# Rotary partners fetched by transfers between partitions, with four smaller moves, in a decoder layer on one core

## Chip, cores and metric

The kernel runs on 1 core of one Trainium2 chip. The metric is device microseconds of one execution, as the median of several.

## What is computed

One decoder layer over 32 sequences of 128 tokens and width 128, with a context of 77 rows for each sequence.

```python
x = x + attn(layernorm(x), rotary on q and k, 16 heads of 8, softmax) @ Wp + bp
x = x + cross_attn(layernorm(x), ctx)              # 16 heads of 8, 77 keys
x = x + ffn(layernorm(x))
# rotary: q*cos + rot(q)*sin, rot swaps the two features of each pair and negates one
# ffn: top 2 of 8 experts (128 -> 512 -> 128, gelu), weighted by a softmax of the two
#      logits, then layernorm(input + sum) * gamma + beta
```

## The kernel before

Features lie on partitions for the projections, tokens on partitions for everything between. Sequences are taken in 8 groups of 4, so that a projection is one product over 512 columns.

**The 64 steps.** One loop over STEPS does attention. A step is one sequence of self-attention or one of cross-attention; from step 13 to step 50 the two kinds alternate, then only cross-attention is left. Each engine has its own program of the same steps, and `plan()` (L97) is the table that says in which step a group's other work falls: `put` places a product with its evictions in a step and a turn (ITEMS), `job` a piece of work of SP, ACT, DVE or POOL (JOBS). All engines work in order. They meet at semaphores alone.

In a step n, TensorE (PE) does, in order: `shifted(st, 0)`, which writes the shifted scores of two of four row tiles and beside them the raw scores of step n+2; `rows_turned` of step n-2 (L891); filler products where the step has no projection (`dense`, L978, 3 or 6 of them); the turned maxima of step n+1 (L879); the second half of the values of step n-1 (L873); the items of turn 1 (projections, L921 among them); `projected` of step n-2 (L898, L899); `shifted(st, 1)`; `sums_turned` of step n-1 (L886); filler; the first half of the values of step n. `sums_turned` waits for ACT's copy of the sums and, because it writes where the projection was, for DVE's residual of step n-2 (L1346).

In a step DVE does: two maxima of step n+2 (L1319), its part of the items of turn 1, the residual of step n-2, two more maxima, `norm_rows` of step n-1 (L1328, L1330), which waits for `sums_turned` and is what `rows_turned` of the next step waits for, and then the statistics of step n-2. ACT does two exponentials (L1140), some copies, its part of the items, and two more exponentials.

**Rotary.** For each group g and for q and k there are two products over 512 columns: one with the weights, one with the weights' columns swapped in pairs (`rq`, `rk`). DVE adds the bias to each and multiplies with the cosine or the sine (L1368), out of PSUM into `ra` and `rb`. POOL adds the two (`turned`, L1775), ACT makes the high half in f16 (`high_part`), POOL the low half (`low_part`, L1780), and SP parks both in DRAM and spreads them over the rows that the scores need (`park_q`, `spread_q`, L627 and L637). For groups 4 to 7 the q product is in step 11, 18, 26 and 34 and the k product in the step behind it; the sum is in the same step, high, low and park one and two steps later, the spread three steps later.

**Hand-over.** In the last steps the first 40 tiles of the experts are laid out: the routed rows of group 5 are scattered to DRAM by POOL (L1860), two in each of the steps 60 to 63 (place 0 and 1 in `scatters`), and DVE builds the table `tab` in four pieces, the last one (`first_entries`, L1507 to L1479) at the start of step 63. SP loads a tile of 128 routed rows (L721) only when all scatters of groups 4 and 5 have landed and `tab` is there. PE turns a loaded tile (L1080), DVE copies it, and the expert's products follow (L1069, L1095), three tiles deep; `expert_turns` drives all engines, `between(i)` puts the rest of the attention between the turns.

**Last stage.** Eight chunks of four sequences: PE sums the two expert outputs of each token into one of eight PSUM banks (L1121), DVE takes statistics (L1688, L1691) and the negated mean (L1693), POOL makes the inverse deviation and the product (`inverse_deviations`, L1956 to L1960), ACT normalizes (L1289), DVE, and POOL in chunks 1 and 3, multiplies with gamma (L528), and DVE adds the rest (L1711).

Of the kernel before, what the change touches and what calls it, by code (L numbers as in the profile page):

```python
# [30 lines left out]
GS = 4  # L31
# [39 lines left out]
BETA = 3  # L71
NA = ((EARLY + 1) * TOK * TOPK - E * (P - 1)) // P // ROUND * ROUND
# [28 lines left out]
def plan():  # L101
# [14 lines left out]
    for g in range(NG):  # L116
        own = SELF_STEP[g * GS + GS - 1]
        if g >= 2:
# [17 lines left out]
            job(made + 2 if g == 3 else made + 3, "spread", g)  # L136
# [27 lines left out]
        if chosen < NS:  # L164
# [5 lines left out]
            for i in range(GS):  # L170
                for k in range(TOPK):
                    job(chosen + 1 + i, ("scatter", k), (g, i, k))
# [33 lines left out]
def decoder_layer(nc, x, ctx_t, w_self, b_self, bp, w_cross, b_cross, bo, wg, bg, w1, b1, w2, b2,  # L206
# [3 lines left out]
    with stack:  # L210
# [230 lines left out]
        s_rhi = sem("s_rhi")  # L441
        s_route = sem("s_route")
# [80 lines left out]
        LAST = CHUNKS - 1  # L523

# [72 lines left out]
        def _(sp):  # L597
# [88 lines left out]
            for n in range(NS):  # L686
# [18 lines left out]
                for g in jobs_at(n, "load_x"):  # L705
                    load_x(g)
                if n == 20:
# [64 lines left out]
        def _(pe):  # L772
# [211 lines left out]
            def step(st):  # L984
# [114 lines left out]
            def between(i):  # L1099
                if i == -3:  # L1100
# [17 lines left out]
            for n in range(CHUNKS):  # L1118
# [6 lines left out]
        def _(act):  # L1125
# [41 lines left out]
            def work(name, g):  # L1167
                bank, c = item(name, g)
                w = BANKS[bank]
                if name in ("q", "rq", "k", "rk", "log", "pos", "cnt"):  # L1170
                    return
                act.wait_ge(s_w[bank], c)
                if name == "xnt":
# [111 lines left out]
            for i in range(SEQS):  # L1285
                if i % FC == 0:
                    act.wait_ge(s_rsfm, i // FC + 1)
                r = SUM[i // FC][:, (i % FC) * D:(i % FC + 1) * D]
                act.activation(xn3all[:, i * D:(i + 1) * D], r, ACT.Identity,  # L1289
# [3 lines left out]
        def _(dve):  # L1293
# [63 lines left out]
            def work(name, g):  # L1357
# [4 lines left out]

# [185 lines left out]
            def step(st):  # L1548
# [33 lines left out]
                if st.at == COUNTED + 2:  # L1582
                    first_sums()
# [101 lines left out]
            def chunk_statistics(n):  # L1685
                dve.wait_ge(s_add, n + 1)
                for i in range(FC):
                    V.bn_stats(stf[:, n * FC + i, :], SUM[n][:, i * D:(i + 1) * D]).then_inc(s_rawf, 1)  # L1688
# [3 lines left out]
                dve.wait_ge(s_stf, (n + 1) * FC)  # L1692
                V.tensor_scalar(nmf[:, n * FC:(n + 1) * FC], mvf[:, n * FC:(n + 1) * FC, 0], -1.0, None, ALU.mult).then_inc(s_nmean, 1)  # L1693
# [33 lines left out]
        def _(pool):  # L1727
# [42 lines left out]
            def turned(g, k):  # L1770

                for name in (("q", "rq"), ("k", "rk"))[k]:
# [270 lines left out]
```

## Time and profile before

| | |
|---|---|
| median of 3 runs | 603.55 us (601.19 to 603.73) |
| the profiled execution | 598.75 us |
| its span, first to last instruction | 596.9 us |
| busy, share of the span: PE, PE's weight load, DVE, POOL, ACT | 87%, 65%, 65%, 58%, 54% |
| start of step 0, of step 63, of the first expert product, of the last stage's first sum | 28.6, 376.2, 389.7, 565.4 us |

The span is that of the profiled execution. Microseconds in the text count from its start. An engine's idle time has a cost only where PE or another engine of the chain waits for what comes late.

### The profile page before, as it was taken

Reading aid. Unit: us, or ns where it says so; the run is one execution under the profiler, and the core shown is the slowest. Engines: PE = TensorE matmul, PEld = TensorE weight load, DVE = VectorE, ACT = ScalarE, POOL = GpSimd, SP = SyncE. Lnnn points to the kernel's source line nnn. Section 1 sums busy time; section 2 is a strip of 40 time slices with the busy share of each in tenths; the row PEclk is TensorE's granted clock in tenths of the full one; section 3 lists DMA queues with packets and bytes.
Section 4 is the critical chain, followed back from the end, with each engine's and each line's share of the span. In section 5 each row is a group of like instructions: output and inputs, shape, how many; then the busy total and the mean of one; then the engine's idle time right before and its main releaser. Section 6 shows DMA issues by size and latency. Waiting matters only on the chain.

```text
span 596.9 us, 21959 instructions
## 1 busy us (share of the span) xinstructions
PE 519.3 (87%) x7657; PEld 389.0 (65%) x7658; DVE 385.3 (65%) x1275; ACT 324.3 (54%) x870; POOL 347.1 (58%) x475
## 2 busy tenths in 40 slices
PE   6889998989998998888979998789888899999980
PEld 4456565656655655665657676588877799999530
DVE  5778887777886786685855766544644444445096
ACT  2447565766766666665656465445434455555143
POOL 5748597636438748638573467546554554444374
PEclk8999999999999999999999999889999999999995
DMA  5232340431762403403112210022222222222393
GB/s 155 84 115 71 104 152 28 151 91 52 226 230 87 137 20 87 137 25 102 34 40 74 80 47 25 28 55 60 64 68 80 74 69 57 57 57 59 98 252 88
DMA packets 68785, 52.57 MB, mean 88 GB/s; under 512 B 8752, under 2 KB 65077, under 8 KB 68690
## 3 DMA queue, kind: packets, MB, share of 16 engines
q1 hardware_dynamic: 62994, 41.92, 25.1%
q0 software_dynamic: 4352, 8.53, 4.4%
q8 instruction: 59, 0.97, 0.7%
q10 hardware_dynamic: 1344, 0.85, 0.5%
q14 instruction: 36, 0.29, 0.2%
HBM read 33.10 MB, written 18.64 MB: 87 GB/s over the span
## 4 chain that ended last, share of the span: by engine, by line
PE 57%; issue 11%; DVE 9%; DMA 7%; ACT 6%; SPq 5%; POOL 4%; DVEq 0%; ACTq 0%; POOLq 0%
PE S L1069 8%; PE AV L873 7%; PE AV L1095 4%; PE SM L1095 4%; PE ST L841 4%; PE W L921 4%; PE ST L847 4%; PE SM L886 3%; ACT prob L1140 3%; PE AV L978 3%; PE SM L898 2%; DVE nmp L1319 2%; SPq L637 2%; PE W L934 2%; PE SM L891 2%
## 5 line engine op out<-in xcount | busy, mean ns | idle before, releaser
L1140 ACT ACTIVATE prob<-ST 128x512 f32<-128x512 f32 (+1 forms) x256 | 138.4, 592 | 117.3 <-PE ST L847 111.1
L1319 DVE TENSOR_REDUCE nmp<-S 128x4 bf16<-128x308 f32 (+1 forms) x251 | 134.6, 576 | 15.8 <-PE S L797 10.0
L1269 ACT ACTIVATE va<-S,b1s 128x128 f32<-128x128 f32 x284 | 81.1, 369 | 81.0 <-PE S L1069 66.8
L1931 POOL DMA_INDIRECT expert_out<-va,ks x71 | 70.0, 985 | 73.4 <-DVE va L1644 44.7
L1860 POOL DMA_INDIRECT routed<-pay,dest x64 | 65.9, 1029 | 33.3 <-PE ST L847 20.2
L873 PE MATMUL AV<-prob,va 77*32 77x128 f32 (+1 forms) x2048 | 84.4, 280 | 0.6 <-issue 0.5
L1069 PE MATMUL S<-va 128*128 128x128 f32 x568 | 77.7, 280 | 7.6 <-issue 5.5
L841 PE MATMUL ST<-nmt,onesr 32*77 32x128 bf16 (+1 forms) x1024 | 73.7, 219 | 8.9 <-ACT prob L1140 3.3
L1069 PEld LDWEIGHTS S<-va 128*128 128x128 f32 x568 | 70.3, 195 | 10.1 <-issue 8.8
L841 PEld LDWEIGHTS ST<-nmt,onesr 32*77 32x77 bf16 (+1 forms) x1024 | 52.4, 102 | 33.5 <-issue 31.8
L873 PEld LDWEIGHTS AV<-prob,va 77*32 77x32 f32 (+1 forms) x2048 | 49.0, 109 | 24.4 <-issue 20.8
L1828 POOL TENSOR_SCALAR ve<-mv 128x1 f32<-128x1 f32 x64 | 15.7, 245 | 62.2 <-DVE mv L1355 61.7
L886 PE MATMUL SM<-idf,ots 128*128 128x128 f32 x128 | 27.2, 294 | 16.5 <-DVE x L1346 11.3
L1095 PE MATMUL AV<-w2s,va 128*128 x288 | 40.6, 284 | 0.0
L1830 POOL TENSOR_TENSOR rs<-ve,half 128x1 f32<-128x1 f32 x64 | 36.7, 574 | 5.3
L1095 PE MATMUL SM<-w2s,va 128*128 x280 | 39.4, 284 | 0.0
L1644 DVE SCALAR_TENSOR_TENSOR va<-AV,ks 128x128 f32<-128x128 f32 x36 | 12.6, 351 | 40.3 <-remote 15.0
L978 PE MATMUL AV<-onesr,idb 128*128 128x256 bf16 x255 | 38.0, 273 | 0.3 <-ACT x2all L1134 0.3
L847 PE MATMUL ST<-q2s,k2s 32*77 32x128 f16 x512 | 35.8, 214 | 0.0
L1095 PEld LDWEIGHTS AV<-w2s,va 128*128 128x128 f32 x288 | 35.0, 192 | 0.8
L1631 DVE COPY va<-w1s 128x512 f32 x71 | 30.5, 430 | 6.9 <-PE S L1069 5.3
L1095 PEld LDWEIGHTS SM<-w2s,va 128*128 128x128 f32 x280 | 34.0, 192 | 0.7
(278 smaller groups left out, 1133.2 us busy)
## 6 DMA issues: line engine op xcount, KB each, us to landing
ks<-routed SPq DMA_DIRECT2D x72, 65.0 KB
q2s<-q_parts SPq DMA_DIRECT2D x32, 128.0 KB
qs<-q_parts SPq DMA_DIRECT2D x20, 128.0 KB
ks<-k_parts SPq DMA_DIRECT2D x20, 128.0 KB, 2.7
k2s<-k_parts SPq DMA_DIRECT2D x32, 77.0 KB
xin<-x SPq DMA_DIRECT2D x8, 256.0 KB, 3.4
q_parts<-q2part SPq DMA_DIRECT2D x8, 256.0 KB
w1s<-w SPq DMA_DIRECT2D x8, 256.0 KB, 4.4
```

Source lines behind the costliest of these rows:

```text
L841: mm(o, onesr[rows, b, 0:st.keys], nmt[rows, st.at % 2, :], start=True, stop=False)
L847: ins = mm(o, k, q, start=False, stop=True)
L873: last = mm(AV[32 * c:32 * c + 32, m * L:(m + 1) * L], v[0:st.keys, st.group % 2, at:at + VW], prob[0:st.keys, j, b * L:(b + 1) * L], star ...
L886: last = tr(TURNED[:, m * L:(m + 1) * L], ots[:, m * L:(m + 1) * L], idf[:, :])
L978: mm(bank, idb[:, :], some[:, 0:bank.shape[1]], start=True, stop=True)
L1069: last = mm(S[k][:, q * P:(q + 1) * P], w1c[:, k, q * P:(q + 1) * P], xt[:, (c + 1) % 4, :], start=True, stop=True)
L1095: last = mm(o, ht[:, (c - 1) % 4, q, :], w2s[:, bass.ds(e * (HID // D) + q * D, D)], start=False, stop=(q == HC - 1))
L1140: act.activation(prob[0:st.keys, j, :], ST[j % 2][0:st.keys, :], ACT.Exp, scale=SCALE).then_inc(s_exp, 1)
L1269: last = act.activation(ht[:, (c + 1) % 4, q, :], S[k][:, q * P:(q + 1) * P], ACT.Gelu, bias=b1s[:, bass.ds(b + q, 1)])
L1319: V.tensor_reduce(nmp[:, st.at % 2, row_tile(p), 0:NB], bank[:, 0:NB * st.keys].rearrange("p (b k) -> p b k", b=NB), AX.X, ALU.max, negate ...
L1860: pool.indirect_dma_start(out=routed, out_offset=bass.IndirectOffsetOnAxis(ap=dest[:, g % 2, i, k:k + 1].bitcast(U32), axis=0), in_=pay[:, ...
L1931: pool.indirect_dma_start(out=expert_out, out_offset=bass.IndirectOffsetOnAxis(ap=xr[:, at % ROUND, D + 1:D + 2].bitcast(U32), axis=0), in ...
```

## The change

It has five parts.

1. For groups 4 to 7 (SWAP = 4) the products `rq` and `rk` go. ACT moves the q or k product with its bias out of PSUM into `rb`. SP copies it to `ra` with each pair of partitions exchanged, in two transfers of 64 partitions. One step later DVE multiplies `ra` with the sine and `rb` with the cosine (`rotate`, at the end of its step). POOL's sum, the high and low halves, park and spread all come one step later than before.
2. PE's `sums_turned` comes behind filler and values of the step, no longer ahead of them.
3. The scatters of group 5 go three, three and two into the steps 60, 61 and 62; the pieces of `tab` come earlier, the last at the start of step 62.
4. In the first three turns of the experts PE gets two filler products of 512 columns each.
5. In the last stage chunk 0 is summed in two halves, in two banks; the negated mean is made by POOL, no longer by DVE.

```diff
@@ plan()
-                put(at, turn, names[1], g)
+                if g < SWAP:
+                    put(at, turn, names[1], g)
+                else:
+                    job(at, "swap", (g, k))
+                    at += 1
+                    job(at, "rotate", (g, k))
                 job(at, "sum", (g, k))
                 job(at + 1, "high", (g, k))
                 job(at + 2, "low", (g, k))
                 job(at + 2, ("park_q", "park_k")[k], g)
-            job(made + 2 if g == 3 else made + 3, "spread", g)
+            job(made + 2 if g == 3 else made + 3 if g < SWAP else made + 4, "spread", g)
...
+                    n = TOPK * i + k
+                    if g == EARLY:
+                        job(chosen + 1 + n // 3, ("scatter", n % 3), (g, i, k))
+                    else:
+                        job(chosen + 1 + i, ("scatter", k), (g, i, k))
@@ sync
+            def swap(g, k):
+                bank, c = item(("q", "k")[k], g)
+                sp.wait_ge(s_wf[bank], c)
+                sp.wait_ge(s_parts, 2 * (g - 1) + k + 1)
+                sp.dma_start(ra[0::2, k, :], rb[1::2, k, :]).then_inc(s_swap[k], 16)
+                sp.dma_start(ra[1::2, k, :], rb[0::2, k, :]).then_inc(s_swap[k], 16)
@@ tensor, step()
                 shifted(st, 1, after)
+                background(st, 2)
+                values(st, 0)
                 if before:
                     sums_turned(before)
-                background(st, 2)
-                values(st, 0)
@@ tensor, between()
+                if i < 0:
+                    dense(2, ST[1][:, :])
@@ tensor, last stage
-            for n in range(CHUNKS):
+            for m in range(2):
+                at = slice(m * FC // 2 * D, (m + 1) * FC // 2 * D)
+                for k in range(TOPK):
+                    pe.wait_ge(s_y2[k][0], 16)
+                    last = mm((SUM[0], SUM[LAST])[m][:, at], idf[:, :], y2[0][:, k, at], start=(k == 0), stop=(k == TOPK - 1))
+                last.then_inc(s_add, 1)
+            for n in range(1, CHUNKS):
+                if n == LAST:
+                    pe.wait_ge(s_norm, FC)
@@ scalar, work()
+                if name in ("q", "k"):
+                    k = ("q", "k").index(name)
+                    act.wait_ge(s_sum, 2 * (g - 1) + k + 1)
+                    act.activation(rb[:, k, :], w[:, :], ACT.Identity, bias=bqk[:, 2 * k:2 * k + 1]).then_inc(s_wf[bank], 1)
@@ vector
                 if name in ("q", "rq", "k", "rk"):
+                    if g >= SWAP:
+                        return
...
+            def rotate(g, k):
+                dve.wait_ge(s_swap[k], 32 * (g - SWAP + 1))
+                for part, table in ((ra, sinb), (rb, cosb)):
+                    p3 = part[:, k, :].rearrange("p (i l) -> p i l", i=GS)
+                    V.tensor_tensor(p3, p3, table[:, :].unsqueeze(1).to_broadcast([P, GS, L]), ALU.mult).then_inc(s_rot, 1)
@@ vector, step()
                 if st.at == COUNTED + 2:
-                    first_owners()
-                if st.at == COUNTED + 3:
+                    first_sums()
                     first_entries()
...
+                for g, k in jobs_at(st.at, "rotate"):
+                    rotate(g, k)
                 background(st, 2)
                 background(st, 3)
...
                 if st.at == COUNTED + 1:
                     take_tiles()
-                if st.at == COUNTED + 2:
-                    first_sums()
+                    first_owners()
@@ vector, chunk_statistics(): the negated mean goes; gpsimd, inverse_deviations():
-                pool.wait_ge(s_nmean, n + 1)
+                pool.wait_ge(s_stf, (n + 1) * FC)
                 G.tensor_scalar(rsf[:, 1, at], mvf[:, at, 1], 4 * EPS, None, ALU.add).then_inc(s_rsf, 1)
+                G.tensor_scalar(nmf[:, at], mvf[:, at, 0], -1.0, None, ALU.mult).then_inc(s_nmean, 1)
```

On PE, in step 35, where group 7's k is made, before (`xnt,wqk` is the product with the q or k weights, `wcross,onormt` the projection of step 33):

```order
L891 MATMUL SM<-idf,onorm 128x128
L879 MATMUL AV<-idb,nmp 128x128
L873 MATMUL AV<-prob,va 32x128 x8
L921 MATMUL W<-xnt,wqk 128x512 x2
L898 MATMUL SM<-wcross,onormt 128x128
L899 MATMUL SM<-c,three_ones 128x128
```

and now:

```order
L920 MATMUL SM<-idf,onorm 128x128
L908 MATMUL AV<-idb,nmp 128x128
L902 MATMUL AV<-prob,va 32x128 x8
L950 MATMUL W<-xnt,wqk 128x512
L927 MATMUL SM<-wcross,onormt 128x128
L928 MATMUL SM<-c,three_ones 128x128
```

One of the two products of 512 columns ahead of the projection is gone. At the end of the same step, before:

```order
L841 MATMUL ST<-nmt,onesr 77x128 x2
L797 MATMUL S<-k2s,q2s 128x77 x2
L847 MATMUL ST<-q2s,k2s 77x128 x2
L886 MATMUL SM<-idf,ots 128x128 x2
L873 MATMUL AV<-prob,va 32x128 x8
L841 MATMUL ST<-nmt,onesr 128x128 x2
```

and now:

```order
L870 MATMUL ST<-nmt,onesr 77x128 x2
L826 MATMUL S<-k2s,q2s 128x77 x2
L876 MATMUL ST<-q2s,k2s 77x128 x2
L902 MATMUL AV<-prob,va 32x128 x8
L915 MATMUL SM<-idf,ots 128x128 x2
L870 MATMUL ST<-nmt,onesr 128x128 x2
```

The sums' transposition (`idf,ots`) has gone behind the values (`prob,va`), next to the shifted scores of step 36.

On POOL, steps 61 to 63 (`routed` is a scatter; `ve`, `rs`, `pay` are one norm; `gsum` is the first row of the count of group 6, in step 63), before:

```order
L1860 DMA routed<-pay,dest 33920x130 x2
L1828 TENSOR_SCALAR ve<-mv 128x1
L1830 TENSOR_TENSOR rs<-ve,half 128x1
L1841 TENSOR_SCALAR pay<-x2all,mv,rs 128x128
L1860 DMA routed<-pay,dest 33920x130 x2
L1828 TENSOR_SCALAR ve<-mv 128x1
L1830 TENSOR_TENSOR rs<-ve,half 128x1
L1841 TENSOR_SCALAR pay<-x2all,mv,rs 128x128
L1860 DMA routed<-pay,dest 33920x130 x2
L1848 TENSOR_TENSOR gsum<-hotb 128x16
```

and now:

```order
L1893 TENSOR_SCALAR pay<-x2all,mv,rs 128x128
L1912 DMA routed<-pay,dest 33920x130 x3
L1880 TENSOR_SCALAR ve<-mv 128x1
L1882 TENSOR_TENSOR rs<-ve,half 128x1
L1893 TENSOR_SCALAR pay<-x2all,mv,rs 128x128
L1912 DMA routed<-pay,dest 33920x130 x3
L1880 TENSOR_SCALAR ve<-mv 128x1
L1882 TENSOR_TENSOR rs<-ve,half 128x1
L1893 TENSOR_SCALAR pay<-x2all,mv,rs 128x128
L1900 TENSOR_TENSOR gsum<-hotb 128x16
```

The last two scatters of group 5 stood in step 63, directly ahead of the count; now the last two stand ahead of the norm of step 62.

## Rows read from the trace of the kernel before

**Rows 1.** Page, busy time, share of the span, instructions; then granted clock by slices.
```profile
PE 519.3 (87%) x7657; PEld 389.0 (65%) x7658; DVE 385.3 (65%) x1275; ACT 324.3 (54%) x870; POOL 347.1 (58%) x475
...
PEclk8999999999999999999999999889999999999995
```

**Rows 2.** Groups: form, count | busy us, mean ns | idle before, releaser.
```profile
L921 PE MATMUL W<-xnt,wqk 128*128 128x512 f32 x48 | 24.0, 620 | 1.5 <-ACT xnt L1134 1.5
...
L1368 DVE SCALAR_TENSOR_TENSOR rb<-W,bqk,sinb 128x512 f32<-128x512 f32 x14 | 10.5, 748 | 1.4 <-PE W L921 0.5
...
L1192 ACT ACTIVATE q2part<-W,bqk 128x512 f16<-128x512 f32 x8 | 5.5, 687 | 4.9 <-PE W L943 4.9
```

**Rows 3.** Timeline, step 34: start us, us, engine line [idle before].
```profile
217.09 2.06 PE L921 MATMUL W<-xnt,wqk 128*128 128x512 f32 x4
...
218.98 0.38 PE L898 MATMUL SM<-wself,onormt 128*128 128x128 f32 x2
...
219.26 0.74 DVE L1368 SCALAR_TENSOR_TENSOR rb<-W,bqk,sinb 128x512 f32<-128x512 f32 x1
...
220.35 0.41 PE L886 MATMUL SM<-idf,ots 128*128 128x128 f32 x2 [0.37 <-DVE x L1346]
...
221.59 0.29 DVE L1330 TENSOR_TENSOR onorm<-SM,rden 128x128 f32<-128x128 f32 x1
...
221.94 0.33 PE L891 MATMUL SM<-idf,onorm 128*128 128x128 f32 x1
```

**Rows 4.** Waits of PE over the 64 steps: us, times, longest.
```profile
PE SM L886 <- DVE x L1346: 11.3, 19, 1.0
...
PE SM L898 <- ACT onormt L1134: 5.1, 10, 0.9
...
PE SM L886 <- DVE x2all L1346: 3.4, 8, 1.0
```

**Rows 5.** Timeline, step 25, which has filler products and no wait.
```profile
169.34 0.44 PE L886 MATMUL SM<-idf,ots 128*128 128x128 f32 x2
...
169.61 0.49 PE L978 MATMUL AV<-onesr,idb 128*128 128x256 bf16 x3
...
170.25 0.29 DVE L1330 TENSOR_TENSOR onorm<-SM,rden 128x128 f32<-128x128 f32 x1
...
171.17 0.33 PE L891 MATMUL SM<-idf,onorm 128*128 128x128 f32 x1
```

**Rows 6.** Timeline, DVE after steps 19 and 27.
```profile
142.97 0.29 DVE L1346 TENSOR_TENSOR x<-SM,xin 128x128 f32<-128x128 f32 x1 [0.71 <-PE SM L899]
...
183.10 1.29 DVE L1319 TENSOR_REDUCE nmp<-S 128x4 bf16<-128x512 f32 x2 [0.37 <-PE S L797]
```

**Rows 7.** DMA issues: KB, median us to landing.
```profile
ks<-k_parts SPq DMA_DIRECT2D x20, 128.0 KB, 2.7
...
w1s<-w SPq DMA_DIRECT2D x8, 256.0 KB, 4.4
```

**Rows 8.** Timeline, the hand-over to the experts.
```profile
368.92 0.98 POOL L1860 DMA_INDIRECT routed<-pay,dest  x1 [1.14 <-PE ST L847]
...
380.20 0.23 DVE L1479 CAST tab<-x2t 1x160 int32<-1x160 f32 x1
...
380.77 0.41 PE L886 MATMUL SM<-idf,ots 128*128 128x128 f32 x2 [1.45 <-DVE x2all L1346]
...
387.10 0.45 PE L1080 MATMUL W<-idf,ks 128*128 128x128 f32 x1 [2.16 <-DMA ks<-routed]
...
389.65 0.77 PE L1069 MATMUL S<-va 128*128 128x128 f32 x2 [0.98 <-DVE va L1631]
```

**Rows 9.** Chain that ended last, 376 to 396: start us, us, what.
```profile
380.16 3.88 DMA routed<-pay,dest
...
384.19 0.49 SPq L720
```

**Rows 10.** Windows: PE, PEld, DVE, ACT, POOL busy, then granted clock.
```profile
388.00:392.00 4.00, 2.83 (x12) 2.56 (x13) 1.56 (x6) 0.00 (x0) 2.05 (x2) 0.50 0.37 89
```

**Rows 11.** Timeline, the last stage.
```profile
570.46 0.17 DVE L1693 TENSOR_SCALAR xnt<-xnt 128x4 f32<-128x4 f32 x1
...
574.81 1.27 POOL L528 TENSOR_TENSOR xn3all<-xn3all,gammar 128x512 f32<-128x512 f32 x1
...
574.93 1.17 DVE L1693 TENSOR_SCALAR xnt<-xnt 128x4 f32<-128x4 f32 x1
...
576.19 0.70 POOL L1956 TENSOR_SCALAR xnt<-xnt 128x4 f32<-128x4 f32 x1
...
586.93 0.59 POOL L1956 TENSOR_SCALAR xnt<-xnt 128x4 f32<-128x4 f32 x1 [0.33 <-DVE xnt L1693]
```

**Rows 12.** One line, all its instructions: ns min/median/max.
```profile
L1711 DVE TENSOR_TENSOR x2all<-xn3all,x2all x9: 424/691/693, 573.0 to 591.8; 128x512 f32<-128x512 f32 x7, 128x256 f32<-128x256 f32 x2
```

More of the change, by code:

```diff
@@ L71 @@
 BETA = 3
+SWAP = 4
 NA = ((EARLY + 1) * TOK * TOPK - E * (P - 1)) // P // ROUND * ROUND
@@ L441, in decoder_layer @@
         s_rhi = sem("s_rhi")
+        s_swap = [sem(f"s_swap{k}") for k in range(2)]
+        s_rot = sem("s_rot")
         s_route = sem("s_route")
@@ L523, in decoder_layer, with summed @@
         LAST = CHUNKS - 1
+        def summed(i):
+            bank = SUM[LAST] if FC // 2 <= i < FC else SUM[i // FC]
+            return bank[:, (i % FC) * D:(i % FC + 1) * D]
         def times_gamma(eng, first, seqs, s):
@@ L706, in _ @@
                     load_x(g)
+                for g, k in jobs_at(n, "swap"):
+                    swap(g, k)
                 if n == 20:
@@ L1169, in work @@
                 w = BANKS[bank]
-                if name in ("q", "rq", "k", "rk", "log", "pos", "cnt"):
+                if name in ("rq", "rk", "log", "pos", "cnt") or name in ("q", "k") and g < SWAP:
                     return
                 act.wait_ge(s_w[bank], c)
-                if name == "xnt":
+                if name in ("q", "k"):
+                    k = ("q", "k").index(name)
+                    act.wait_ge(s_sum, 2 * (g - 1) + k + 1)
+                    act.activation(rb[:, k, :], w[:, :], ACT.Identity, bias=bqk[:, 2 * k:2 * k + 1]).then_inc(s_wf[bank], 1)
+                elif name == "xnt":
                     move(turned_of(g)[:, :], w[:, :], s_wf[bank])
@@ L1287, in _ @@
                     act.wait_ge(s_rsfm, i // FC + 1)
-                r = SUM[i // FC][:, (i % FC) * D:(i % FC + 1) * D]
-                act.activation(xn3all[:, i * D:(i + 1) * D], r, ACT.Identity,
+                act.activation(xn3all[:, i * D:(i + 1) * D], summed(i), ACT.Identity,
                                bias=rsf[:, 1, i:i + 1], scale=rsf[:, 0, i:i + 1]).then_inc(s_norm, 1)
@@ L1685, in chunk_statistics @@
             def chunk_statistics(n):
-                dve.wait_ge(s_add, n + 1)
-                for i in range(FC):
-                    V.bn_stats(stf[:, n * FC + i, :], SUM[n][:, i * D:(i + 1) * D]).then_inc(s_rawf, 1)
+                for i in range(n * FC, (n + 1) * FC):
+                    dve.wait_ge(s_add, n + 2 if n or i >= FC // 2 else 1)
+                    V.bn_stats(stf[:, i, :], summed(i)).then_inc(s_rawf, 1)
                 dve.wait_ge(s_rawf, (n + 1) * FC)
@@ L1770, in turned @@
             def turned(g, k):
-                for name in (("q", "rq"), ("k", "rk"))[k]:
-                    bank, c = item(name, g)
-                    pool.wait_ge(s_wf[bank], c)
+                if g >= SWAP:
+                    pool.wait_ge(s_rot, 2 * (2 * (g - SWAP) + k + 1))
+                else:
+                    for name in (("q", "rq"), ("k", "rk"))[k]:
+                        bank, c = item(name, g)
+                        pool.wait_ge(s_wf[bank], c)
                 G.tensor_tensor(ra[:, k, :], ra[:, k, :], rb[:, k, :], ALU.add).then_inc(s_sum, 1)
@@ L1865, in scatters @@
                 for g, i, k in jobs_at(n, ("scatter", place)):
-                    pool.wait_ge(s_st[1], NJ // 2 * n + place + 1)
+                    pool.wait_ge(s_st[1], NJ // 2 * n + min(place, 1) + 1)
                     scatter(g, i, k)
@@ L1902, in step @@
                     norm_instance(near(st, -2))
+                scatters(n, 2)
             set_up()
```

4 lines of the change are left out of this document (1 added, 3 removed).

## The prediction

> **What bounds the kernel now.** The page comes first: TensorE (PE) is busy 519.3 us, 87% of the span, and its granted clock is at or near the upper level almost everywhere [rows 1]. So work taken off PE counts in full where PE waits for nothing, and each stretch where it waits has to be read by itself.
>
> For the groups of columns I go to the grouped lines [rows 2]. For the cost of a product I go to the timeline of a step with a rotary product [rows 3]. There both products together (four matmuls) begin at 217.09, and the projection L898 begins at 218.98: PE advances 1.89 us for two, 0.95 us each by the starts and 1.03 by the row's own 2.06; I take 0.97. Behind them the same rows show the second limit. DVE does the second bias and sine out of PSUM, 0.74 us, then the residual, and `sums_turned` (L886) waits 0.37 us for it. The waits over the 64 steps [rows 4] say how often that is: 11.3 us at 19 self steps, 3.4 us at 8 cross steps, and 5.1 us at 10 steps for ACT's `onormt`. In a step with filler and no items [rows 5] PE waits for neither; DVE's norm (L1330) ends at 170.54 and `rows_turned` (L891) starts at 171.17.
>
> Last come the seams: the hand-over to the experts, where PE waits 1.45 us behind DVE's table pieces and 2.16 us for the first routed tile [rows 8], where the chain of waits goes over the last scatter [rows 9] and the clock is 0.50 [rows 10]; and the last stage, where PE is done early and POOL and DVE alternate [rows 11, 12].
>
> **Part 1, eight products less.** 8 x 0.97 = **-7.7 us** [rows 3]. DVE has cover for what comes in their place, with two exceptions:
> - ACT's move with bias: the nearest row is a bias eviction of the same size, 0.69 us [rows 2]. It starts when the product ends, and PE has about 1 us of projection and shifted scores before it needs the bank's or ACT's next result. Nothing.
> - The swap on SP: an issue took 0.49 us [rows 9], so 1.0 us for two. A spread of 128 KB landed in 2.7 us, a load of 256 KB in 4.4 us [rows 7]. From the product's end to `rotate` I count 0.7 + 1.0 + 2.7 to 4.4, that is 4.4 to 6.1 us. DVE comes to `rotate` at the end of the next step: that step begins near 221.94 [rows 3] and takes 5.5 us (64 steps in 353) or a little more, so about 228, 9 us behind the product's end at 219.15. Hidden. POOL's sum, the halves, park and spread come one step later, but group 4's spread then stands in step 15, and its scores are first wanted in step 18, where the later groups have more. Nothing.
> - The two multiplies on DVE. What they replace, two passes of 748 ns [rows 2], lay in front of the residual; they lie at the end of the step, in front of the next maxima. I have no row of a multiply of 128x512 that reads SBUF alone but L1711 of the last stage, an addition: 691 ns [rows 12]. So 1.4 us at each of eight places. Behind steps 19 and 27 DVE has 0.71 and 0.37 us of idle time [rows 6], elsewhere more. The rest is late for the maxima, the residual and so the sums: 1.3 us for group 4, 0.9 for group 5, 0.4 for each of the last two. **+3.0 us.** Bounds: 0 (all in idle time) and 8 x 1.4 = +11.
>
> A rule speaks against the form of the swap. By the Trainium skill ("DMA: Bandwidth & Descriptors", "Rules for kernel authors") two transfers to disjoint halves of the partitions serialize, and one of 128 partitions should be used. No row of this trace has such a pair; by the rule the second lands 2.7 us behind the first, and the sum above does not change, since 7 to 9 us would still be just inside the step.
>
> **Part 2, sums behind filler and values.** In the 8 cross steps of rows 4 the residual is awaited while values could run: -3.4 us. At the 19 self steps nothing is gained. There DVE's chain (residual, maxima, norm, L1328 to L1330) is itself what `rows_turned` waits for: in rows 3 the norm ends at 221.88 and L891 starts at 221.94. In the 28 steps with filler the sums go up to 1.0 us later, and their end plus DVE's 0.76 us for reciprocal and norm then exceeds the old start of L891 by 0.27 us: in rows 5, 171.17 against sums ending near 170.6 plus 0.8 and the hand-overs. 28 x 0.27 = 7.6 us; at the 10 places where PE waits 5.1 us for `onormt` behind ACT's exponentials [rows 4] it is absorbed, about 3. So +4.5 - 3.4 = **+1 us**, with -3 (none of the 7.6) to +6 (a little more than all of it, less the gain).
>
> **Part 3, scatters and table.** The last scatter of group 5 is issued at 380.16 and lands 3.88 us later; then SP issues the tile's load [rows 9], PE waits 2.16 us for it, and PE has waited 1.45 us for the residual, which stands behind the last table cast at 380.20 [rows 8]. With the last scatters one step (5.5 us) earlier they are issued by 374.7 and land at 378.6; the table comes before 375. Both waits are then gone, -3.6. A third scatter at the end of steps 60 and 61 is 1.1 us more on POOL, which idles 1.14 us ahead of the second scatter there [rows 8]. The table pieces stand in front of a residual one step earlier: some of the 1.45 stays. With the four filler products and the clock, which is 0.50 from 384 to 392 [rows 10] behind those waits, I come to **-3.8 us**. Bounds: -2 (only the tile's wait) and -5.6 (clock back early as well).
>
> **Part 4, filler in three turns.** PE waits for a tile or for DVE's copy there (0.98 us before 389.65 [rows 8]), so it lies in idle time; 0, at most 3 x 0.3 = +1. It is in the bounds of part 3.
>
> **Part 5, last stage.** From 572 on, POOL's inverse deviations set the pace: 0.23 to 0.70 us for a small operation [rows 11]. The negation is one more such, 0.2 us or so, in each of six chunks, less the 0.33 us that POOL still waits for DVE at 586.93. But 0.17 us (and 1.17 us, in chunks beside POOL's gamma) go from DVE. Chunk 0 in halves starts the stage sooner by half of its sums, in a stretch where POOL has nothing: taken back later by POOL. **+0.8 us**, bounds -1 and +2.
>
> **The sum.** -7.7 + 3.0 + 1 - 3.8 + 0.8 = -6.7. Against the profiled execution of 598.75 us, whose span is 596.9 us, that is 592.0 us. The execution is 4.8 us below the median of the runs, 603.55 us; taken off the median it is **596.9 us**.
>
> **The rivals.**
> - **A: DVE waits for the swap (slower).** `rotate` stands in DVE's queue, so whatever follows (maxima, residual, norm) waits with it, then PE. It decides if the two transfers land later than about 9 us behind the product. For: the exchange goes by single partitions, and no row shows one. Against: 4.4 us for the largest load in rows 7. Late by 1.5 us at 8 places is +12 on 596.9: 608.9 us.
> - **B: the multiplies stall against POOL.** L1693, 0.17 us as a rule, takes 1.17 us at 574.93 beside POOL's gamma from 574.81 [rows 11]: a small DVE operation that reads and writes SBUF took 1.0 us longer. The multiplies of `rotate` stand where POOL norms a sequence or adds a pair. At three places +3, 600 us; at all eight 604.9.
> - **C: the sums behind the values cost their full 7.6 us**, gains of waits only on paper: 602.4 us, no change.
> - **D: the hand-over gives nothing**, since the next thing there (the residual behind the logits, or the load of the tile) is as late: 600.6 us.
> - **E: everything that hangs on DVE in part 1 is hidden** and the clock comes back early: -12, 591.5 us.
>
> Rival B has a rule beside it. The Trainium skill ("SBUF — State Buffer", "Who interferes with whom") says that DVE and GpSimd share a port pair as an exclusive lock, and that a DVE operation with two inputs from SBUF holds it. By that rule each `rotate` that meets a POOL operation waits for its end, and the reverse; the trace agrees in kind with its 1.17 beside 0.17 us.
>
> **How the numbers follow.** A measurement of this kernel can tell about 0.5%, 3 us, from no change: faster is below 600.5. The forecast has .68, A .05, B .08, C .08, D .05, E .06. Faster is the forecast's, E and the milder half of B and D: 0.77. Same holds C and the rest of B and D: 0.15. Slower is A and the worst of B and C together: 0.08. The bounds of parts 1 to 5 added as independent give about -5 and +6 around 596.9; the range of 8 in 10 is 590.5 to 603.5.
>
> **What would show it.** Right: L921's successor has 32 matmuls in place of 48; PE's time from 28.6 to the first expert product falls by about 8 us; the wait of L886's successor for the residual in cross steps is gone, while `rows_turned` now waits for `onorm` in filler steps; the multiplies take near 0.7 us with no wait for the swap in front; PE's wait for the first routed tile is gone, and the last chunk's times stay. Wrong: idle time of DVE in front of `rotate` (A); multiplies of over 1 us beside POOL (B); waits of `rows_turned` of 0.3 us and more in most steps (C); a wait before the first tile that is still 2 us (D).

## The result and the profile after

| | before | changed |
|---|---|---|
| median of 4 runs | 603.64 us (601.19 to 604.17) | 628.55 us (617.53 to 633.68) |
| profiled execution, its span | 598.75, 596.9 us | 626.57, 624.7 us |
| mean granted clock of the profiled execution | 0.978 | 0.914 |

The changed kernel is slower: ratio 1.031, 95% interval 1.018 to 1.045. Ratios, here and below, are of the fast runs, those within 1.5% of the fastest of their kernel (here two of the four); by the medians it is 1.041. 596.9 us was forecast, with 590.5 to 603.5 as the range. Its runs are 16 us apart and sorted by clock: 617.53 us at 0.939, 626.57 at 0.914, 630.53 at 0.902, 633.68 at 0.899.

The page of the changed kernel, the rows that answer to [rows 1]:

```profile
PE 553.2 (89%) x7651; PEld 409.4 (66%) x7652; DVE 381.5 (61%) x1267; ACT 331.8 (53%) x878; POOL 348.6 (56%) x483
...
PEclk9999899999999998999589755579999899999996
```

PE issues six instructions fewer and is busy 33.9 us longer. The last row gives most of the reason: in slices 20 and 24 to 26 of 40 the granted clock is near 0.5. The windows around the two longest low stretches (columns as in [rows 10]: stretch, length, busy time and count of PE, PEld, DVE, ACT, POOL, then clock, DMA share, GB/s):

```profile
292.00:298.00 6.00, 5.00 (x92) 2.91 (x90) 5.14 (x16) 2.17 (x5) 4.91 (x11) 1.00 0.17 58
298.00:316.00 18.00, 16.70 (x212) 10.67 (x212) 6.90 (x21) 7.96 (x20) 9.64 (x13) 0.53 0.08 24
344.00:350.00 6.00, 4.62 (x96) 3.29 (x93) 2.87 (x10) 2.48 (x7) 4.18 (x7) 1.00 0.65 177
350.00:382.00 32.00, 31.95 (x366) 21.75 (x364) 13.22 (x56) 11.77 (x29) 14.48 (x22) 0.50 0.07 21
382.00:415.00 33.00, 32.33 (x312) 21.83 (x312) 15.13 (x71) 11.80 (x27) 13.53 (x22) 0.50 0.12 33
```

From 350 to 415 us the clock stands at 0.50, the lower of its two levels, 1.2 GHz. PE is then busy all the time (31.95 of 32 us), DVE for 13.22 us of the same 32. A shorter low stretch is at 298 to 316, and windows of 1 us show three more, of 3 to 4 us, at 66, 186 and 237 (a sixth, at 493, lies in the experts' stage). Just ahead of each of the five the timeline of PE has its longest waits:

```profile
66.05 0.23 PE L870 MATMUL ST<-nmt,onesr 32*128 32x128 bf16 x2 [1.77 <-DMA w1s<-k_parts]
...
185.68 0.25 PE L870 MATMUL ST<-nmt,onesr 32*77 32x128 bf16 x2 [1.22 <-ACT prob L1180]
...
236.32 0.23 PE L870 MATMUL ST<-nmt,onesr 32*128 32x128 bf16 x2 [1.40 <-ACT prob L1180]
...
299.30 0.80 PE L927 MATMUL SM<-wcross,onormt 128*128 128x128 f32 x2 [1.49 <-ACT onormt L1174]
...
348.27 0.33 PE L920 MATMUL SM<-idf,onorm 128*128 128x128 f32 x1 [1.38 <-issue]
```

Where the time went, by stretch (a step is counted from one turned maxima, L879 or now L908, to the next; the differences are of the two profiled executions):

| stretch | changed minus before, us |
|---|---|
| ahead of step 0 | -1.1 |
| 16 of the 64 steps, at and behind the low stretches (6, 7, 29, 30, 37 to 39, 50 to 52, 57 to 62) | +29.2 |
| the other steps | -5.6 |
| from there to the first expert product (18.9 us before, 23.1 now) | +4.2 |
| experts to the first sum of the last stage | +1.4 |
| last stage | -0.3 |
| sum | +27.8 |

So the products did go (32 matmuls of L950 in place of 48), and the eight steps that held them are 7.5 us shorter together. The loss lies elsewhere, at and behind the stretches at low clock.

### The profile page after: what moved, and what is told of

Same layout as the page of the kernel before. It is cut to its first block, busy times and chain, and to the rows that moved or that the text cites. A ratio compares the mean times of both kernels' runs of the same rounds, so it can differ in the third digit from the quotient of the medians.

```text
span 624.7 us, 21971 instructions
## 1 busy us (share of the span) xinstructions
PE 553.2 (89%) x7651; PEld 409.4 (66%) x7652; DVE 381.5 (61%) x1267; ACT 331.8 (53%) x878; POOL 348.6 (56%) x483
## 4 chain that ended last, share of the span: by engine, by line
PE 57%; DVE 12%; issue 8%; DMA 7%; POOL 5%; SPq 5%; ACT 4%; DVEq 1%; POOLq 0%; another core or an unknown queue 0%; ACTq 0%
PE AV L902 9%; PE S L1098 7%; PE AV L1007 5%; DVE nmp L1362 4%; PE ST L870 4%; PE SM L1124 3%; PE AV L1124 3%; PE ST L876 3%; ACT prob L1180 3%; PE SM L927 3%; PE W L950 2%; SPq L656 2%; DMA expert_out<-va,ks 2%; PE SM L920 2%; PE SM L915 2%
## 5 line engine op out<-in xcount | busy, mean ns | idle before, releaser
L870 PE MATMUL ST<-nmt,onesr 32*77 32x128 bf16 (+1 forms) x1024 | 83.3, 232 | 14.7 <-ACT prob L1180 9.7
L902 PE MATMUL AV<-prob,va 77*32 77x128 f32 (+1 forms) x2048 | 92.1, 302 | 0.0
L870 PEld LDWEIGHTS ST<-nmt,onesr 32*77 32x77 bf16 (+1 forms) x1024 | 57.2, 111 | 40.4 <-issue 38.7
L902 PEld LDWEIGHTS AV<-prob,va 77*32 77x32 f32 (+1 forms) x2048 | 52.9, 117 | 24.3 <-issue 14.5
L1880 POOL TENSOR_SCALAR ve<-mv 128x1 f32<-128x1 f32 x64 | 15.3, 239 | 71.1 <-DVE mv L1398 69.4
L1007 PE MATMUL AV<-onesr,idb 128*128 128x256 bf16 x255 | 47.4, 321 | 0.7 <-ACT nmt L1174 0.4
L876 PE MATMUL ST<-q2s,k2s 32*77 32x128 f16 x512 | 43.2, 239 | 0.0
L1371 DVE RECIPROCAL rden<-SM 128x16 f32<-128x16 f32 x64 | 16.2, 253 | 40.5 <-PE SM L915 40.5
L1174 ACT ACTIVATE ots<-AV 128x256 f32<-128x256 f32 x64 | 24.9, 390 | 19.9 <-PE AV L902 19.6
L1686 DVE COPY va<-W 128x128 f32<-128x128 f32 x71 | 20.5, 288 | 24.4 <-PE W L1109 20.3
```

What stands on the lines that cost most here:

```text
L870: mm(o, onesr[rows, b, 0:st.keys], nmt[rows, st.at % 2, :], start=True, stop=False)
L876: ins = mm(o, k, q, start=False, stop=True)
L902: last = mm(AV[32 * c:32 * c + 32, m * L:(m + 1) * L], v[0:st.keys, st.group % 2, at:at + VW], prob[0:st.keys, j, b * L:(b + 1) * L], star ...
L1007: mm(bank, idb[:, :], some[:, 0:bank.shape[1]], start=True, stop=True)
```

## The experiments

Theory T, formed on the profile above: `sums_turned` behind the values (part 2) lets PE's small waits run together, and the clock falls behind them. Rival U: eight products less leave PE too little to do, whatever the order. Rival V: the swaps' traffic makes the waits. Later came rival W: the late sums cost the time by themselves and the clock is only a symptom.

### One part undone, one part alone

`e1_sums_ahead` is the change without part 2:

```diff
@@ tensor, step(), of the changed kernel
-                background(st, 2)
-                values(st, 0)
                 if before:
                     sums_turned(before)
+                background(st, 2)
+                values(st, 0)
```

> The changed kernel with its part 2 undone (sums_turned again ahead of filler and values); parts 1, 3, 4, 5 stay. Theory T (the late sums collect PE's small waits into single ones of 1.2 to 1.5 us, behind which the granted clock falls to 0.50 for up to 63 us): the stretches at 0.50 at steps 29, 37, 50 and 57 go, mean clock back to 0.97 or more, time 594 to 600 us. Rival U (eight products less leave PE too little to do, whatever the order): the clock stays at 0.90 to 0.94 and the time above 612. Rival V (the swaps' DMA traffic makes the waits): the same as U.

`e2_no_swap` is the change without part 1:

```diff
-SWAP = 4
+SWAP = 8
```

> The changed kernel with its part 1 undone (SWAP 8: all products for the partners as before); parts 2 to 5 stay. Theory T: the low stretches at steps 50 and 57, far behind the last swap, stay; mean clock 0.90 to 0.95, time 618 to 640 us. Rivals U and V: clock 0.97, time 600 to 608 us.

`e3_sums_late_only` is the kernel before with part 2 alone (the first diff the other way round, on the kernel before).

> The kernel before with part 2 alone. Theory T: slower by 2 to 5%, 615 to 635 us, with stretches at clock 0.50 in the 64 steps. Rivals U and V: 600 to 608 us, the ledger of part 2 alone (+1 us, at most +6), clock 0.97.

Measured on one chip, where the kernel before took 605.63 us: without part 2 596.97 us (593.39 to 599.92), ratio 0.984 (0.976 to 0.992); without part 1 625.05 us, 1.034 (1.025 to 1.042); part 2 alone 619.12 us, 1.014 (1.005 to 1.022). U and V fall with this as the cause of the loss: with the swaps and the eight products less, but the old order, the kernel is faster than before, and with none of them (e2) it is as slow as the change. The loss needs part 2. Alone it costs 1.4% (2.2% by the medians), where T gave 2% to 5% and 615 to 635 us; the rest of e2's 3.4% comes with parts 3 to 5 beside it, and no run says from which of them. The page of `e1_sums_ahead`:

```profile
PEclk9999999899999899999999999999999999999995
```

Its clock is 0.979, but it isn't free of low stretches. Its windows, and the longest wait of PE in the 6 us ahead of the second:

```profile
107.00:110.00 3.00, 3.00 (x24) 2.42 (x15) 2.97 (x12) 1.55 (x6) 2.05 (x4) 0.50 0.34 91
203.00:209.00 6.00, 5.64 (x74) 3.53 (x73) 4.65 (x19) 2.52 (x5) 1.14 (x3) 0.50 0.25 81
```

```profile
199.65 0.23 PE L870 MATMUL ST<-nmt,onesr 32*128 32x128 bf16 x2 [0.38 <-ACT prob L1180]
```

The profile of the kernel before has no low stretch in its 64 steps. So part 1 may have a price in clock of its own; it is small, since the mean clocks of e1's four runs (0.970 to 0.979) are those of the kernel before (0.961 to 0.980). The waits of PE over the 64 steps of `e1_sums_ahead` (us, times, longest):

```profile
PE SM L915 <- DVE x L1389: 11.2, 16, 1.2
PE ST L870 <- ACT prob L1180: 9.0, 20, 1.4
...
PE SM L915 <- DVE x2all L1389: 2.3, 4, 1.0
```

and of the changed kernel:

```profile
PE ST L870 <- ACT prob L1180: 9.7, 22, 1.4
...
PE SM L915 <- DVE x L1389: 2.3, 5, 0.5
```

The waits for the residual have gone from 11.2 + 2.3 to 2.3 us, as the change promises. What the sum of waits doesn't show is what lies behind the sums. At the start of step 57, before:

```profile
339.19 0.44 PE L886 MATMUL SM<-idf,ots 128*128 128x128 f32 x2
...
339.82 0.25 DVE L1328 RECIPROCAL rden<-SM 128x16 f32<-128x16 f32 x1
...
341.49 0.33 PE L891 MATMUL SM<-idf,onorm 128*128 128x128 f32 x1
...
342.91 0.86 DVE L1319 TENSOR_REDUCE nmp<-S 128x4 bf16<-128x308 f32 x2 [2.03 <-remote]
343.07 1.08 ACT L1140 ACTIVATE prob<-ST 77x512 f32<-77x512 f32 x2 [2.69 <-remote]
```

and changed:

```profile
345.88 0.44 PE L915 MATMUL SM<-idf,ots 128*128 128x128 f32 x2
...
347.63 0.26 DVE L1371 RECIPROCAL rden<-SM 128x16 f32<-128x16 f32 x1 [2.47 <-PE SM L915]
...
348.27 0.33 PE L920 MATMUL SM<-idf,onorm 128*128 128x128 f32 x1 [1.38 <-issue]
...
348.60 1.08 ACT L1180 ACTIVATE prob<-ST 77x512 f32<-77x512 f32 x2 [2.87 <-remote]
```

In both kernels DVE and ACT stand idle here for 2.0 to 2.9 us; the trace puts three of the four idle times down to "remote" and names no queue or engine. Of the fourth (2.47 us, changed) DVE spends the last 1.3 us with its input ready: the sums end at 346.32. Before, the norm was over by then (it followed the sums of 339.19), so that PE ran `rows_turned` (341.49) and the rest through the pause. With the sums behind the values the norm comes 1.3 us behind them, and `rows_turned` waits 1.38 us. That is the wait ahead of the 65 us at clock 0.50.

A wait of this length isn't enough by itself, nor is it needed: in e1 the clock fell behind 0.38 us. The kernel before has a wait of 1.43 us at step 11, and its clock stays at 1.00:

```profile
92.00 0.23 PE L841 MATMUL ST<-nmt,onesr 32*128 32x128 bf16 x2 [1.43 <-DMA q2s<-q_parts]
```

What tells these cases apart isn't settled by any run.

### Filler in the waits

If the clock were all, filler products in the five waits would bring the time back while every other engine is as late as before. `f1_fill_five`:

```diff
@@ tensor, step(), of the changed kernel
                 shifted(st, 0, after)
+                if st.at == 57:
+                    dense(8, AV[:, 2 * L:4 * L])
                 if last:
                     rows_turned(last)
...
-                    dense(idle_at(st, 1), AV[:, 2 * L:4 * L])
+                    dense(idle_at(st, 1) + (6 if st.at == 49 else 0), AV[:, 2 * L:4 * L])
...
                 if before:
                     sums_turned(before)
                 background(st, 3)
+                if st.at in (5, 28, 36):
+                    dense(7, AV[:, 2 * L:4 * L])
```

> The changed kernel, late sums and all, with about 1 us of filler products more for PE at the five places where its profile shows a wait of 1.2 us or more just ahead of a stretch at clock 0.50: 7 filler products at the end of steps 5, 28 and 36, 6 ahead of step 49's turned maxima, 8 ahead of step 57's rows_turned. Theory T (the single long wait brings the clock down, the low clock costs the time): the stretches at 0.50 there are gone or short, mean clock 0.96 or more, 596 to 605 us, though no wait of another engine has been shortened. Rival W (the late sums cost the time by themselves, the clock is a symptom): 615 us or more.

`f2_fill_one` has the first of these edits alone.

> The changed kernel with filler at the last of the five places alone (8 products ahead of step 57's rows_turned), where its profile shows the longest low stretch, 350 to 415 us. Theory T: that stretch goes, the other four stay: 605 to 616 us. Rival W: 622 us or more.

They came to a chip on which the kernel before took 581.83 us, 4% less. There f1 took 586.97 us, 1.008 (1.001 to 1.014), and f2 582.37 us, 1.001 (0.996 to 1.007): no answer, since the change itself wasn't run beside them. What differs is in the traces: on this chip no wait of ACT or DVE is put down to "remote" (in the kernel before, on the other chip, 9.0 us of ACT's and 19.9 of DVE's are). I call these chips with and without pauses. So the change went beside its variants twice more.

On a chip without pauses (the kernel before: 579.53 us):

> The changed kernel, unedited, beside its variants on one chip. The last four runs were on a chip whose traces show none of the pauses put down to 'remote' and where the kernel before takes 582 us. Theory T (late sums turn pauses of the other engines into waits of PE, and these bring the clock down): on a chip with pauses 617 to 635 us and clock 0.90 to 0.95; on one without, 578 to 590 us, within 1.5% of the kernel before and clock 0.96 or more. Rival W (late sums are slow by themselves): 3% over the kernel before on any chip.

> The change with the sums ahead again (as before: 0.984 of the kernel before on a chip with pauses). Theory T: 0.98 to 0.995 of the kernel before on either chip, faster than the change by 3 to 5% with pauses, by 0 to 1.5% without.

> The change with filler at five places. Theory T: with pauses 0.985 to 1.005 of the kernel before, well under the change on the same chip; without pauses no better than the change, up to 1% worse, since there is no wait left to fill. Rival W: no better than the change on any chip.

> The change with filler ahead of step 57's rows_turned alone. Theory T: with pauses about half of the way from the change to the kernel with five fillings, 605 to 616 us; without pauses the same as the change within 1%.

The change took 574.68, 579.34, 593.08 and 603.30 us, at clocks of 0.986, 0.979, 0.961 and 0.933: from as fast as before to 4% slower, and again sorted by clock; the median, 586.21 us, is 1.2% over the kernel before's. With the sums ahead (g2) 577.48 us, 0.997 (0.993 to 1.001); five fillings (g3) 585.10 us, 1.004 (0.999 to 1.010); one (g4) 584.20 us, 1.009 (1.005 to 1.013). This is what T asked for, but for g2's ratio (0.98 to 0.995 expected): the loss shrinks where there are no pauses, and there is nothing for the filler to win.

On a chip with pauses (the kernel before: 601.57 us):

> The changed kernel once more beside its variants. Theory T with chips of two kinds: on one whose traces show pauses of ACT and DVE put down to 'remote' (the kernel before then takes 600 us or more) 1.02 to 1.05 of the kernel before, mean clock under 0.95; on one without (580 us) 0.99 to 1.015.

> The change with filler at the five places. Theory T: with pauses at least half of the change's loss comes back (1.02 or less of the kernel before, clock 0.955 or more); without pauses 1.00 to 1.01. Rival W: the same as the change on a chip with pauses too.

> The change with the sums ahead. Theory T: 0.98 to 0.99 of the kernel before with pauses, 0.995 to 1.00 without (0.9969 measured there).

The change 616.60 us, 1.023 (1.012 to 1.034); five fillings 612.39 us, 1.019 (1.012 to 1.026); sums ahead 601.52 us (590.54 to 601.94), 2.4% under the change by the medians, where e1 and the first comparison, on two chips, differ by 5%. Against the kernel before that is 1.00 by the medians, and T's 0.98 to 0.99 is missed: one run took 590.54 us at a clock of 0.984, three took 601.4 to 601.9 us at 0.956 to 0.966. The profile of such a run has the clock at 0.50 from 247 to 270 us, with the sums ahead. The old order makes low stretches rarer; it doesn't rule them out. A stretch at low clock of the change, and what is there with filler, by windows of h1 and of h2:

```profile
298.00:320.00 22.00, 21.87 (x280) 14.04 (x281) 9.08 (x28) 9.29 (x24) 11.22 (x16) 0.53 0.20 56
```

```profile
290.00:300.00 10.00, 8.70 (x176) 5.49 (x173) 8.80 (x34) 5.31 (x14) 4.66 (x11) 1.00 0.10 32
300.00:356.00 56.00, 48.46 (x946) 33.94 (x943) 31.85 (x114) 31.94 (x79) 29.02 (x46) 1.00 0.22 61
```

The filler did what it was put in for: from 290 to 356 us the clock is 1.00, and h2's runs have clocks of 0.959 to 0.973 where h1's have 0.912 to 0.954. It brought back 4 us of 15 by the medians, less than the half that T asked for (its ratio, 1.019, and its clock are inside what was written beside that), and the intervals of h1 and h2 overlap. The filler isn't free either: the group of L1007 is busy 43.1 us up to 385 us in h2's profile and 38.8 in h1's. So h2 doesn't measure what the low clock costs. It shows that most of the loss stays with the clock held up, as W has it; how much of that is the late sums and how much the filler itself stays open.

### What the late sums cost at full clock

The two kernels g1 and g2 differ by part 2 alone, on a chip without pauses. By steps, g1 is 9.9 us longer over the 64 (335.1 against 325.2 us). 22 steps are longer by 0.17 to 0.45 us, 5.9 us together; steps 21, 47, 49, 50, 57 and 61 by 0.6 to 1.4 us, and two low stretches (273 to 277, 290 to 294) lie at 47 and 50; some are shorter by up to 0.7 us. PE's waits, g2 first; the last row of each is from the view of `rows_turned` (L920), whose weights PE loads ahead of the matmul, and counts both:

```profile
PE SM L915 <- DVE x L1389: 10.6, 15, 1.1
PE ST L870 <- ACT prob L1180: 4.0, 13, 0.4
...
PE SM L915 <- DVE x2all L1389: 2.2, 3, 1.0
...
PE S L826 <- DVE nmp L1362: 0.4, 2, 0.2
...
  DVE onorm L1373: 2.4, 12
```

```profile
PE ST L870 <- ACT prob L1180: 6.5, 21, 0.4
...
PE S L826 <- DVE nmp L1362: 3.3, 15, 0.6
PE SM L915 <- DVE x L1389: 2.4, 5, 0.5
...
  DVE onorm L1373: 11.4, 39
```

10.4 us of waits for the residual went. 2.5 us for ACT's exponentials and 2.9 us for DVE's maxima came, and `rows_turned` now waits for DVE's norm 39 times, in place of 12. PE's busy time over the 64 steps rose from 294.9 to 305.2 us with as many instructions. 8.6 us of that are in the shifted scores and the raw scores beside them (L870, L876 and L826), where one matmul takes as long as before (214 to 222 ns): they start further apart. DVE's chain from the sums over the norm to `rows_turned` starts later, and what hangs on it is late with it.

### Part 3, and what is left of the change

`f3_no_handover` and `h4_hand_third` (one kernel) are parts 1 and 5 alone:

```diff
@@ plan(), of the changed kernel with the sums ahead
-                    if g == EARLY:
-                        job(chosen + 1 + n // 3, ("scatter", n % 3), (g, i, k))
-                    else:
-                        job(chosen + 1 + i, ("scatter", k), (g, i, k))
+                    job(chosen + 1 + i, ("scatter", k), (g, i, k))
@@ vector, step(): first_owners(), first_entries() and first_sums() where they were
@@ tensor, between()
-                if i < 0:
-                    dense(2, ST[1][:, :])
```

> Parts 1 and 5 of the change alone: the sums ahead again, scatters two a step, the table's pieces where they were, no filler in the first three turns. If part 3 is worth its 3.8 us, this is that much slower than the kernel with parts 1, 3, 4 and 5 (597.0 us): 600 to 602 us. If the hand-over gives nothing: 596 to 598 us.

> Parts 1 and 5 alone. If the third scatter's delay of POOL's norms (PE waited 2.40 us for pay in place of 1.06 us, and the clock was 0.50 for 22 us in place of 14) is what part 3 costs, this is 0.3 to 1% faster than the change with the sums ahead, on either kind of chip. If the hand-over's own gain of 3.4 us counts, it is 0.5% slower.

0.992 of the kernel before both times: 575.43 us against 581.83 (0.987 to 0.996), 597.23 us against 601.57 (0.989 to 0.995). With part 3, sums ahead, it was 0.984, 0.997 and, by the medians, 1.00 in the third comparison; `f4_negation_dve` had part 3 too and was 0.998 (0.994 to 1.003) where f3 was 0.992. So on both chips where kernels with and without it ran, the one with it is 0.7% slower (the intervals of f3 and f4 overlap by a little); e1's 0.984 stands on a chip where no kernel without it ran. The rows say how it can lose. With part 3 (g2), PE's wait ahead of the group's `x3t` and the windows around:

```profile
355.91 0.63 PE L976 MATMUL W<-idf,pay 128*128 128x128 f32 x4 [2.40 <-POOL pay L1893]
```

```profile
356.00:364.00 8.00, 8.00 (x74) 6.24 (x75) 2.55 (x19) 2.62 (x5) 4.62 (x6) 0.55 0.11 33
364.00:378.00 14.00, 13.68 (x111) 8.81 (x110) 5.60 (x26) 4.52 (x11) 5.28 (x12) 0.53 0.14 35
```

and without (f3):

```profile
354.69 0.63 PE L972 MATMUL W<-idf,pay 128*128 128x128 f32 x4 [1.06 <-POOL pay L1889]
```

```profile
356.00:364.00 8.00, 6.55 (x111) 5.11 (x106) 5.16 (x31) 4.23 (x10) 4.69 (x6) 1.00 0.08 25
364.00:378.00 14.00, 10.81 (x71) 8.12 (x69) 5.75 (x25) 4.30 (x13) 6.09 (x12) 0.51 0.22 54
```

The third scatter of a step stands in POOL's queue in front of the norm that writes `pay`, and PE waits 2.40 us for it, in place of 1.06. Behind that wait the clock is near 0.5 from 356 us on; without part 3 it holds until 364. From the last turned maxima to the first expert product it is 23.6 us in g2 and 19.9 in f3. In e1, where the clock held there, it was 15.3 us, and before 18.9: the gain of 3.6 us is real there (the step ahead of it is 1.0 us longer), and is lost with the clock.

`f4_negation_dve` put the negated mean back on DVE.

> Parts 1, 3, 4 of the change and the halved first chunk, the negated mean back on DVE, the sums ahead. By the ledger the negation on POOL costs 0.3 to 1.5 us: 595.5 to 597 us against 597.0; the rival, that DVE's 1.17 us beside POOL's gamma made it worth moving, gives 597.5 to 599 us. Small beside the noise; the profile of the last stage decides.

579.79 us: by the time it tells nothing of so small a term. The last stage of its profile is 31.6 us, that of f3's, with the negation on POOL, 31.2. Three more kernels on the chip of the h runs (602.85 us before this time): the table early but two scatters a step (i1), part 1 alone (i2), parts 1 and 5 (i3).

> Parts 1 and 5 of the change and of part 3 only the earlier table pieces; the scatters of group 5 stay two a step. The residual's wait behind the table (1.45 us) should go and POOL's norms stay on time (PE's wait for pay at 1.1 us, not 2.4): 0 to 0.4% faster than i3. If the table itself was what cost, 0.5% slower.

> Part 1 alone: the partners by transfers, all else as before. By the measured steps (8 products of 0.95 us, less 0.5 to 1 us of DVE) 0.985 to 0.993 of the kernel before on either kind of chip; part 5 is then worth less than 0.2% either way.

> Parts 1 and 5, for the comparison on the same chip: 0.992 of the kernel before, as measured twice.

598.93 us, 0.993 (0.990 to 0.997); 599.98 us, 0.993 (0.988 to 0.998); 599.21 us, 0.995 (0.992 to 0.999). They can't be told apart. Part 1 carries all of the gain that is left, and the table and part 5 are worth nothing that shows. Nor is part 1 alone safe: one run of i2 took 610.03 us, and its profile has the clock at 0.50 from 346 to 372 us.

## Why the prediction was wrong

**The bound and part 1 were right.** The eight steps with the products of groups 4 to 7 are shorter by 0.86 to 1.06 us, 7.5 together, and 7.9 in every profile of part 1 with the sums ahead; -7.7 was forecast. ACT's move took 0.69 us as taken from the row of a like eviction. Of DVE's +3.0 us a part came. Step 15 is 0.9 us longer in g2, and 0.9 to 1.6 in every kernel with part 1: there group 4's multiplies stand in front of the maxima and the residual (1.3 us were forecast for this group).

```profile
107.07 0.68 DVE L1437 TENSOR_TENSOR rb<-rb,cosb 128x512 f32<-128x512 f32 x1
...
110.06 0.26 DVE L1389 TENSOR_TENSOR x<-SM,xin 128x128 f32<-128x128 f32 x1
...
110.46 0.41 PE L915 MATMUL SM<-idf,ots 128*128 128x128 f32 x2 [1.06 <-DVE x L1389]
```

In step 21, where 0.9 us were forecast for group 5, it is 0.2; for groups 6 and 7 the profiles can't be read, as pauses and clock differ there. As a whole part 1 gained 0.7%, some 4 us (i2), where -4.7 was forecast; some of the eight steps' 7.9 us is lost again in other steps, in which the profiles of e1 and i2 have the low stretches named above. The changed kernel's rows for group 7's q, from the product to the two multiplies, and the durations of all sixteen:

```profile
216.32 1.10 PE L950 MATMUL W<-xnt,wqk 128*128 128x512 f32 x2
...
217.47 0.69 ACT L1216 ACTIVATE rb<-W,bqk 128x512 f32<-128x512 f32 x1 [0.63 <-PE W L950]
...
218.18 0.51 SPq L672 DMA_DIRECT2D ra<-rb  x1
...
218.74 0.59 SPq L673 DMA_DIRECT2D ra<-rb  x1
...
225.06 0.66 DVE L1437 TENSOR_TENSOR ra<-ra,sinb 128x512 f32<-128x512 f32 x1
...
225.64 0.68 DVE L1437 TENSOR_TENSOR rb<-rb,cosb 128x512 f32<-128x512 f32 x1
```

```profile
L1437 DVE TENSOR_TENSOR ra<-ra,sinb x8: 656/658/689, 103.2 to 230.5; 128x512 f32<-128x512 f32 x8
L1437 DVE TENSOR_TENSOR rb<-rb,cosb x8: 678/684/686, 103.8 to 231.1; 128x512 f32<-128x512 f32 x8
```

From the product's end (217.42) to the second issue's (219.33) it is 1.9 us, to `rotate` 7.6, where I had 9. In none of the 16 multiplies did DVE wait for a swap. Rival A is out. The Trainium skill warns against two transfers to halves of the partitions, since they serialize ("DMA: Bandwidth & Descriptors", "Rules for kernel authors"); here that cost nothing, the median from issue to landing of the 16 was 2.1 us. Rival B is out too: 656 to 689 ns in all of them, eight of which ran beside an operation of POOL. The Trainium skill's lock between DVE and GpSimd ("SBUF — State Buffer", "Who interferes with whom") shows in no row of `rotate`. Nor was the row of 1.17 us, on which the prediction leaned for it, such a case: L1693 reads one tile from SBUF, a multiply of `rotate` two.

**Part 2 is the step that failed, twice over.** I wrote +4.5 - 3.4 = +1 us, with +6 as the upper end. Where nearly nothing of the clock is lost (g1 against g2) it is +9.9. The 0.27 us a step were right: 22 steps of 0.17 to 0.45 us, 5.9 us, where I had 7.6 for 28 steps. The gain of 3.4 us came in part: eight steps are shorter, by 2.5 us together. The residual's wait went, and waits for the norm, the maxima and the exponentials behind it took its place, as they hang on the same chain. What had no term are the 6.1 us of six more steps (21, 47, 49, 50, 57 and 61), two of which hold a low stretch of 3 to 4 us. I had rival C for a late chain, at 602.4 us, and gave it 8 in 100. The larger failure is that the clock stood in the prediction only at the hand-over, where the profile already had it at 0.50. I read 0.978 and a wait of 1.43 us without harm as safety. There was no rival in which the waits, moved together, bring the clock down elsewhere, and the range had no room for one. The changed kernel's profile has the clock at 0.50 for some 90 us of the 64 steps and the hand-over, and the 16 steps at these stretches lose 29.2 us.

**Part 3** was right in its mechanism: forecast at -3.8, it is -3.6 us where the clock holds (15.3 against 18.9 us). I costed the third scatter at 1.1 us on an idle POOL and did not name who waits behind it: the norm whose `pay` PE turns. This and the clock take the gain back.

**Part 5:** from the first sum of the last stage to the end 31.2 us, 31.5 before; -0.3 against +0.8 forecast, inside the bounds. The negation on POOL (L2010) is 0.23 us in two chunks, as forecast, and 0.62 to 0.65 us in the six others; the addition ahead of it (L2009, before L1956) fell from 0.60 to 0.23 us as a median, so that the two together are some 0.25 us longer.

**The chances.** With the order of part 2 undone the change measured 596.97 us on one chip, the number that was forecast for all five parts, and 0.997 and 1.00 on two others. That agreement is luck. Without part 2 the sum is -7.7 us; e1 gained some 10 us by its ratio of 0.984, with 5 to 14 as the interval, g2 2 us and h3 none. The whole change, for which -6.7 was forecast, lost 19 us by its ratio.

## What to carry to other kernels

Moving a wait is not removing it: before an operation is put behind filler, follow the chain that starts at it (here sums, reciprocal, norm, turned rows) and ask what PE has left to run when the other engines pause. In a kernel whose PE runs at the upper clock, and waits often, give the fall of the clock a rival of its own, priced by what the next tens of microseconds would cost at the lower level, because the spread of the runs follows it (617.5 to 633.7 us here, 574.7 to 603.3 on another chip). Compare variants on one chip: one and the same kernel differed by 4% from chip to chip.

## What was not expected of the hardware

- Chips differ: the same kernel before took 602 to 606 us in four comparisons and 580 to 582 us in two, on other chips. On the slower ones ACT and DVE stand idle now and then for 1 to 3 us with no releaser of this core named ("remote" in the waits, 2.69 us at 343.07 before), the one of step 57 in the kernel before, in the change and in e1 alike; on the faster ones no such wait is in the trace. What causes them stays open; no experiment was made on it.
- In the changed kernel the granted clock fell to 0.50 behind or in single waits of PE of 1.22 to 1.77 us, and stayed there for 3 to 4 us three times, for 17 and for 65 us, though PE was busy throughout the longest (31.95 of 32 us). In `e1_sums_ahead` it fell behind a wait of 0.38 us, and behind one of 1.43 us in the kernel before it did not fall. So the length of one wait doesn't tell. Why the clock came back at 316 after so short a time and not until 415 the second time isn't shown by any run.
- An indirect scatter holds POOL's queue for some 1.0 us. The third in a step made PE wait 1.3 us longer for the norm that stands behind it (2.40 against 1.06 us).
